# Two attentions and two expert layers on one core: gathers issued eight tiles ahead, fp32 shared up products, spline-weight pieces split between GpSimd and VectorE

## What is computed

```python
# x: (2, 16, 64, 128) = 2048 tokens of 128
# layer 0: x += local attention(layernorm(x)); x += Gelu experts(layernorm(x))
attn = softmax(einsum(q, kw) + pos_bias)          # 8 heads, window of 7 keys
hs = gelu(t @ sw1.T + sb1); shared = hs @ sw2.T + sb2       # 2 shared experts, 128 -> 512 -> 128
probs = softmax(t @ gate_w.T + gate_b); top_v, top_i = top_k(probs, 2)
hr = gelu(t @ rw1[e].T + rb1[e]); oe = hr @ rw2[e].T + rb2[e]  # 8 routed experts
# layer 1: x += window attention(layernorm(x)) with mask and pos_bias;
#          x += spline experts(layernorm(x)), 8 experts, two chosen per token
spline = einsum('nic,oic->no', b_splines(x), spline_w * scaler[..., None])
```

## Time and profile before

| | us |
|---|---|
| median of 3 runs | 1081.29 |
| lowest, highest | 1079.32, 1101.76 |
| the profiled execution | 1086.91 |
| its span in the profile | 1085.1 |
| TensorE busy | 859.6 (79%) |
| VectorE busy | 600.0 (55%) |
| ScalarE busy | 594.8 (55%) |
| GpSimd busy | 396.6 (37%) |
| moved by DMA | 157.42 MB, mean 145 GB/s |

### The profile page before, as it was taken

One profiled execution on the slowest core, in us unless ns is written; L12 is line 12 of the kernel. 1 busy time (PEld: TensorE's weight loads), 2 busy tenths in 40 slices (PEclk: granted clock), 3 DMA queues, 4 the chain that ended last, 5 costly groups with the idle time before them and its releaser, 6 DMA issues. The chain is left out here.

```text
span 1085.1 us, 22519 instructions
## 1 busy us (share of the span) xinstructions
PE 859.6 (79%) x7570; PEld 797.7 (74%) x7570; DVE 600.0 (55%) x1362; ACT 594.8 (55%) x1697; POOL 396.6 (37%) x407
## 2 busy tenths in 40 slices
PE   4684699754656534885698999999999999999993
PEld 3573588644545533674455999999999999999993
DVE  4563564331211344443393687887777777777762
ACT  4785443211212215885103878777777777777751
POOL 3997000343533423999001133233322333232111
PEclk9976599887988875666588999999999999999997
DMA  9362710246563349252506246442245353431000
GB/s 361 133 277 121 262 51 29 73 132 229 182 255 119 125 156 388 100 224 111 191 1 258 110 143 227 138 167 77 97 143 207 118 185 99 146 126 20 9 7 7
DMA packets 39171, 157.42 MB, mean 145 GB/s; under 512 B 5193, under 2 KB 23154, under 8 KB 31938
## 3 DMA queue, kind: packets, MB, share of 16 engines
q1 hardware_dynamic: 29746, 146.36, 36.1%
q0 software_dynamic: 9360, 10.23, 4.9%
HBM read 119.81 MB, written 36.77 MB: 144 GB/s over the span
## 5 line engine op out<-in xcount | busy, mean ns | idle before, releaser
L1472 PE MATMUL kan_ps_h<-kan_xf,kan_w 128*128 128x128 f32 x2496 | 304.3, 275 | 2.0 <-DMA kan_w<-w_dram 2.0
L1472 PEld LDWEIGHTS kan_ps_h<-kan_xf,kan_w 128*128 128x128 f32 x2496 | 291.2, 192 | 2.8 <-DMA kan_w<-w_dram 2.8
L1486 PE MATMUL kan_ps_y<-kan_w,kan_hf 128*128 128x128 f32 x1248 | 154.2, 277 | 8.3 <-DVE kan_hf L1624 8.3
L1486 PEld LDWEIGHTS kan_ps_y<-kan_w,kan_hf 128*128 128x128 f32 x1248 | 147.4, 194 | 8.8 <-issue 8.8
L1695 POOL DMA_INDIRECT out<-kan_y_sb,kan_slots_y x39 | 63.9, 1638 | 230.9 <-ACT kan_y_sb L1570 230.9
L796 ACT ACTIVATE f_hid<-f_ps_up,f_wt 128x128 f32<-128x128 f32 x156 | 44.5, 367 | 151.6 <-PE f_ps_up L737 151.6
L1616 DVE TENSOR_TENSOR kan_hfar<-kan_ht,kan_hfar 128x1024 f32<-128x1024 f32 x39 | 47.8, 1227 | 84.4 <-ACT kan_hnear L1533 84.4
L367 ACT ACTIVATE a_probs<-a_logits,a_below 128x70 f32<-128x70 f32 (+1 forms) x256 | 85.9, 351 | 0.0
L818 POOL DMA_INDIRECT y_dram<-f_y_sb,f_target x39 | 42.2, 1081 | 108.8 <-DVE f_y_sb L972 84.7
L1519 ACT ACTIVATE kan_ht<-kan_hu,kan_biases 128x256 f32<-128x256 f32 x156 | 66.2, 496 | 13.5 <-DVE kan_hu L1643 13.5
L811 POOL DMA_INDIRECT f_slot_x<-normed_dram,f_source x39 | 39.5, 1012 | 91.2 <-DVE f_source L952 79.6
(11 more groups left out here) (257 smaller groups left out, 1896.1 us busy)
## 6 DMA issues: line engine op xcount, KB each, us to landing
kan_w<-w_dram SPq DMA_DIRECT2D x16, 2304.0 KB, 8.9
sw_raw<-in_experts SPq DMA_DIRECT2D x8, 3456.0 KB, 12.4
f_wt<-in_experts SPq DMA_DIRECT2D x39, 514.0 KB
w_dram<-sw_raw SPq DMA_DIRECT2D x8, 2304.0 KB, 7.3
kan_w<-w_dram SPq DMA_DIRECT2D x16, 1152.0 KB, 5.2
w_dram<-sw_raw SPq DMA_DIRECT2D x8, 1152.0 KB, 11.2
sw_scal<-in_scalers SPq DMA_DIRECT2D x8, 384.0 KB, 13.4
f_ws<-in_experts SPq DMA_DIRECT2D x2, 514.0 KB, 4.2
```

What stands on the lines that cost most here:

```text
L1472: mm = eng.matmul(ps_h[n % 2][:, m, :], w12[n % 2][:, at:at + P], rhs, start=(c == 0), stop=(c == BASES))
L1486: mm = eng.matmul(ps_y[n % 2][:, :], lhs, w3[n % 2][:, i * P:(i + 1) * P], start=(i == 0), stop=(i == CH1 * FEAT - 1))
```

## The change

Five parts. (1) In the routed tiles GpSimd gathers eight tiles before it scatters one, with six buffers instead of four, and the gather stands ahead of the scatter in the loop. (2) The shared up products are one fp32 matmul instead of three fp32r passes; the splits on VectorE and ScalarE fall away, as do TensorE's wait for the small bias load. (3) The counts are made one step earlier, ahead of `go_down(0)`, and the lists three steps earlier. (4) In each attention GpSimd does two pieces an iteration (experts 0 and 2, then 5 and 7) and VectorE one (expert 1, then 6); stores 3 and 4 move to the start of the second attention, whose loads 6 and 7 wait for them. (5) The window bias table is made by GpSimd ahead of the second attention instead of by VectorE between routed tiles, and `w1` is loaded a block earlier.

```diff
-        X_BUFFERS = 4
+        X_BUFFERS = 6
...
-        COUNT_AT = 2
-        LIST_AT = STEPS - 1
+        COUNT_AT = 1
+        LIST_AT = 4
...
-                        for j, (wj, nj) in enumerate(PARTS):
-                            mm = eng.matmul(ps_up[c % 2][:, :], w_parts[e][wj][:, c * P:(c + 1) * P],
-                                            n_parts[nj][:, g * GROUP:(g + 1) * GROUP, :],
-                                            start=(j == 0), stop=(j == len(PARTS) - 1))
-                        mm.then_inc(up, 1)
+                        eng.matmul(ps_up[c % 2][:, :], ws[e][:, c * P:(c + 1) * P],
+                                   nT[:, g * GROUP:(g + 1) * GROUP, :], start=True, stop=True).then_inc(up, 1)
...
-                for n in range(X_BUFFERS):
+                for n in range(X_BUFFERS + 2):
                     gather_x(n)
                 eng.wait_ge(slots_ok, 1)
                 for n in range(SLOT_TILES):
+                    gather_x(n + X_BUFFERS + 2)
                     scatter_y(n)
-                    gather_x(n + X_BUFFERS)
...
                 for n in range(SLOT_TILES):
-                    if n < 9:
-                        prep.piece(eng, 3, 2 * n)
...
+                    if n < 2 * prep.PIECES:
+                        prep.piece(eng, 3 + n // prep.PIECES, n % prep.PIECES)
...
+    def gpsimd(self, eng, i):
+        for j in range(2 * (i - self.first), 2 * (i - self.first) + 2):
+            k, piece = divmod(j, self.prep.PIECES)
+            if 0 <= k < len(self.by_gpsimd):
+                self.prep.piece(eng, self.by_gpsimd[k], piece)
+
+    def vector(self, eng, i):
+        if 0 <= i - self.first < self.prep.PIECES:
+            self.prep.piece(eng, self.by_vector, i - self.first)
...
+                          Beside(prep, first=2, by_gpsimd=(0, 2), by_vector=1), x_arrivals=s_x)
...
                 def load1(eng):
-                    eng.dma_start(w1_sb[:, :], d["w1"]).then_inc(s_w1, 16)
...
+                    eng.dma_start(pos1[:, :, :], d["pos1"]).then_inc(s_tab, 16)
+                    eng.dma_start(mask1[:, :, :], d["mask1"]).then_inc(s_tab, 16)
                     prep.load(eng, 5)
+                    prep.store(eng, 3)
+                    prep.store(eng, 4)
+                    prep.load(eng, 6, 3)
+                    prep.load(eng, 7, 4)
...
+                          Beside(prep, first=3, by_gpsimd=(5, 7), by_vector=6, ahead=add_masks), stats)
```

More of the change, by code:

```diff
@@ L388, in _ @@
                     eng.memset(v[b][:, :, :], 0.0).then_inc(zeroed, 1)
+                beside.ahead(eng)
                 arrived(eng)
@@ L476, in _ @@
                     add_out(i - 6)
+                    beside.vector(eng, i)
                 eng.wait_ge(measured, TILES)
@@ L516, in gelu_experts @@
         nT = sb("nT", [P, TILES, P])
-        n_parts = [sb(f"n_part{j}", [P, TILES, P], F32R) for j in range(2)]
         shared_sum = nT
@@ L635, in _ @@
                 eng.dma_start(normed_dram[TOKENS:, :], xn[:, 0, :]).then_inc(saved, 16)
+                eng.wait_ge(zeroed, W_BUFFERS + 1)
+                eng.dma_start(shared_b2[0:SHARED, :], d["b2"][0:SHARED, :]).then_inc(s_b2, 16)
+                for s in to_clear:
+                    eng.sem_clear(s)
+                prep.load(eng, 3)
+                prep.load(eng, 4)
                 eng.wait_ge(lots_ok, 1)
@@ L644, in _ @@
                        .then_inc(in_w[n % W_BUFFERS], 16)
-                    if n == 14:
-                        prep.store(eng, 3)
-                    if n == 22:
-                        prep.load(eng, 4, 3)
                 for i in range(Y_BUFFERS):
@@ L1008, in _, with __init__, ahead @@
                 eng.wait_ge(measured, TILES)
+class Beside:
+    def __init__(self, prep, first, by_gpsimd, by_vector, ahead=None):
+        self.prep, self.first, self.by_gpsimd, self.by_vector = prep, first, by_gpsimd, by_vector
+        self.before = ahead
+    def ahead(self, eng):
+        if self.before is not None:
+            self.before(eng)
+    def gpsimd(self, eng, i):
[6 more added lines that the diff above has]
+            self.prep.piece(eng, self.by_vector, i - self.first)
 class SplineWeights:
@@ L1775, in load0 @@
                     eng.dma_start(pads0[:, :, :], d["pads0"]).then_inc(s_w0, 16)
-                    prep.load(eng, 0)
-                    prep.load(eng, 1)
-                    prep.store(eng, 0)
-                    prep.load(eng, 2, 0)
-                    prep.store(eng, 1)
-                    prep.store(eng, 2)
+                    for e in range(3):
+                        prep.load(eng, e)
+                    for e in range(3):
+                        prep.store(eng, e)
                     for e in range(3):
@@ L1853, in fill1, with add_masks @@
                 def fill1(eng, logits):
-                    pass
-                def beside1(eng, i):
-                    for j in range(3 * (i - 3), 3 * (i - 2)):
-                        if 0 <= j < 3 * prep.PIECES:
-                            prep.piece(eng, 5 + j // prep.PIECES, j % prep.PIECES)
+                    eng.wait_ge(s_biased, WINDOWS // 2)
+                def add_masks(eng):
+                    eng.wait_ge(s_tab, 32)
+                    shape = [P, PAIRS, 2, BLK]
+                    for n in range(WINDOWS // 2):
+                        eng.tensor_tensor(window_bias[:, n, :, :].rearrange("p (h b) k -> p h b k", b=2),
+                                          pos1[:, :, :].unsqueeze(2).to_broadcast(shape),
+                                          mask1[:, 2 * n:2 * n + 2, :].unsqueeze(1).to_broadcast(shape), ALU.add)\
+                           .then_inc(s_biased, 1)
                 w = {n: w1_sb[:, i * P:(i + 1) * P] for i, n in enumerate(("wq", "wk", "wv", "wo"))}
```

152 lines of the change are left out of this document (50 added, 102 removed).

## The result

The changed kernel takes 1017.2 us (median of 4 runs, 1016.4 to 1019.5) against 1080.3 for the kernel before: a ratio of 0.943, with a 95% interval of 0.940 to 0.946. The forecast was 1026, in a range of 994 to 1058. Some executions of a kernel take some per cent longer at a lower granted clock (of e1, one takes 1115.9 us at 0.853 and another 1079.8 at 0.885); the ratios, and the time given for the first experiment, leave them out.

A forecast was written before the change was run, and what follows sets the result against it. Late gathers, queued behind scatters waiting for y, were taken to bound the routed tiles, and GpSimd the attentions. Gelu layer -92, first attention +12, second +25 make -55, so 1081.3 becomes 1026 us, range 994 to 1058.

The forecast's parts named there:

- GpSimd is: Routed tiles: GpSimd is the next bound, 70 operations x 1.27 = 89 us, over TensorE's 83 us.
- above L = 6: Routed tiles, rival (b): L, a weight load's time until it lands, binds above 6 us; 1103 or more, chance 0.04.
- if L727 waits for `f_wt`: Routed tiles: a named sign that the prediction is wrong, line L727 waiting for the weights `f_wt`; no size given.
- GpSimd busy over 85% there: Routed tiles: expected sign in the changed profile, GpSimd over 85% busy with y rows 2.6 to 2.9 us apart.
- The 11 us of collisions: Routed tiles: scatters collide with VectorE's pieces, 0.3 us a tile (between 0 and 0.46), 11 us in all.
- 89 + 11: Routed tiles: GpSimd's 70 operations, 89 us, plus 11 us of collisions with VectorE, giving 100 us.
- The bounds of this sum, 103 and 65: Routed tiles, gain of 90: 103 without collisions and TensorE's 83 us carrying it, 65 at 3.3 us a tile.
- Rival (a): Routed tiles: the low clock keeps the gain, 4.24 us a tile, layer gains about 29, time 1089; chance 0.06.
- nothing gained, nothing lost: Shared part: a step's eight fp32 instructions take 3.47 us against 3.43 for twelve fp32r passes, no change at 2.4 GHz.
- I take 4.65 a tile, hardly better than 4.68: First attention: tile interval 4.65 us (bounds 4.3 and 4.9), as GpSimd's and VectorE's pieces collide.
- would delay the start by 8: Second attention: GpSimd's table work, 10 us, hides in VectorE's wait for a load; uncovered it delays the start by 8.
- the 5.6 us of the profiled execution over its median: Sum: the profiled execution before, 1086.9, is 5.6 over the median, so -55 is taken from 1081.3, giving 1026.

The follow-up runs named there:

- e1: Changed kernel with only GpSimd's order in the routed tiles put back: four gathers ahead, then scatter(n) and gather(n+4), six buffers kept; 1088.0 us, ratio 1.010.
- e5: Changed kernel with five buffers for the routed weights instead of four; 1018.6 us, ratio 0.935.
- e9: Changed kernel with only the first eight gathers (later tiles compute on rows left in the buffers) and five routed weight buffers; 1003.6 us, ratio 0.925.
- e3: Changed kernel without VectorE's 36 pieces of experts 3 and 4 in the routed tiles, whose weights are stored unscaled; 1021.4 us, ratio 0.936.
- e4: Changed kernel with only the first eight gathers, tiles 8 to 38 computing on rows that stay in the buffers; 1022.5 us, ratio 0.936.
- e6: Changed kernel with all three experts of each attention on GpSimd, none on VectorE; loads, stores and tables in the changed kernel's order; 990.5 us, ratio 0.912.
- e8: As e7, with VectorE's pieces in iterations 5 to 16, three in two iterations, and GpSimd's share and the last stores' order changed; 1000.4 us, ratio 0.920.
- e10: Changed kernel with its split of pieces, but VectorE's first-attention pieces from iteration 4, stores and loads reordered, five weight buffers; 990.4 us, ratio 0.912.
- e13: As e10, with GpSimd's normalise ahead of add_bp, VectorE's pieces from iteration 5 in both attentions, store 6 last, beside route; 978.6 us, ratio 0.903.
- e7: Changed kernel with store 3 behind routed tile 26 and load 6 behind the loads of the results, instead of in the second attention; 1012.1 us, ratio 0.933.
- e2: Changed kernel with four row buffers and a lead of six tiles instead of six buffers and eight tiles; 1023.4 us, ratio 0.938.

## Why the prediction was right, and where not

**The bound and the routed tiles.** Right in the main: the order of GpSimd's queue made the gathers late, and without that edit no gain is left (e1), though the other edits of this layer took some 28 us of the stretch by themselves, for which the prediction has no term. Foreseen 107.5 us, and 2 more for stretches at the low clock, to the loads of the results; measured 305.4 - 200.57 = 104.8. The reason given for the 2.6 us a tile was half of it. The step "GpSimd is" the next bound failed: the weight loads bind beside it. The prediction lets them bind "above L = 6", but they do at 4.8 us from issue to use, since its sum for four tiles leaves out the 0.9 us between the down product and the issue, and the waits themselves. Its own sign of being wrong, "if L727 waits for `f_wt`", came in 23 of 39 tiles (the trace names no releaser; e5 and e9 tell it), and its "GpSimd busy over 85% there" did not: 68.98 of 95 us from 205 to 300, 73%. The 11 us of collisions were charged to a path that does not feel them (e3). That 89 + 11 came out at the right length is luck: the load's way over four buffers has nearly the same one. Only e4, e5 and e9 together tell the two apart. The bounds of this sum, 103 and 65, do not follow from its terms: 39 x 2.12 + 7.5 = 90.2 would be a gain of 109, 39 x 3.3 + 7.5 = 136.2 one of 63. The measured 94 lies inside either pair.

**Clock.** Rival (a) fell: the granted clock of the routed stretch is 1.00, against 0.83 before and 0.89 in e1, which has the waits again. So the 2 us for low-clock stretches were not needed. The profiles give the granted clock as a share of full speed only, and the prediction's GHz are in no run; its two states are: eight instructions of an up product take 1.06 us and 1.92 us.

**Shared part.** 82.9 us to the first routed product instead of 84.6, so -1.7; foreseen -2. That is luck: two errors cancel in it. The step "nothing gained, nothing lost" failed: I compared the busy time of a step of before, 3.43, which has its last product's tail in it, with a rate from start to start, 3.47. Like by like a step's eight instructions are busy 3.85 us and twelve passes 3.43, so eight steps cost 3.4 us more.

```profile
161.89 3.85 PE L676 MATMUL f_ps_up<-f_nT,f_ws 128*128 128x512 f32 x8
```

So the other edits of this part saved about 5 us, not 2; which of them, no run here separates.

**First attention,** +5.4 for +12, at the edge of its bounds; the other profiles of the same block give +4.6 to +11.4, so part of the difference is the one execution. The wait was as forecast (the load lands at 27.76, "about 27"). First transposes at 36.13, 1.7 later than the 34.4. The end is 19.3 us behind the last transposes, for 21.0. The step that failed is the interval: "I take 4.65 a tile, hardly better than 4.68" against a measured (98.36 - 36.13)/15 = 4.15, and 4.10 to 4.50 over all nine profiles. I had counted GpSimd's saving of 1.23 us and then given it all to collisions. What the runs give for the same block is 4.69 with three pieces on GpSimd (e6), 4.89 with two and one and a half (e8), and with two and one at a free start 4.51 (e10), no less than behind the wait. If a piece of VectorE held GpSimd up for its own 0.68 us, 3.45 + 0.68 would be 4.13 (an estimate), the low end of the 4.10 to 4.50; the 4.65 went beyond it. No row of the prediction shows what a piece costs GpSimd: its 1.41 us are of `norm`, which has one tensor operand, where a piece has two. In e13 a `normalise` that began under a piece took 1.50 us instead of 1.04. And a collision need not cost time: e3 takes away the scatters' (at most 998 ns instead of 1499), and its tile takes 2.63 us for 2.60.

**Second attention,** +22.8 for +25. VectorE's piece starts 41.6 us after the block's start for 40, the first transposes 47.8 for 45, the last 115.7 for 117.8, and the end is 20.7 behind them for 21.2. The interval is 4.53 instead of 4.9 in the mean, of which 4.9 is right up to the tenth tile and 3.9 holds behind it. The prediction gives no reason for the 4.9 but the 4.96 of before; in the trace it is the loop, and e13 shows that GpSimd's and VectorE's mutual waits would hold it at 4.65 without one. That GpSimd's table work without cover "would delay the start by 8" is not borne out: in e6, where no piece of VectorE waits, the first transposes come 28.6 us after the block's start against 25.4 before, 3.2 later. In e7 they come at 32.5, but there the table work itself begins 7.9 us after the start instead of 4.3, waiting for the mask, whose load is queued behind load 6. The 117.8 for the last transposes is a slip: 45 + 14 x 4.9 + 4 is 117.6.

**The sum.** -67.7 on the span for -55: 4 us of the difference come from the Gelu layer, 6.6 from the first attention (in most other profiles less), 2.2 from the second. Of these 12.7 us the median shows 9 (1026 against 1017.2): I took the 5.6 us of the profiled execution over its median as lasting, and the changed kernel's is over it by 2.3 only.

## What to carry to other kernels

A gather with a queue that also waits for results must stand ahead of that wait (put back behind it, the routed stretch takes 171.6 us for 105.5, e1); how many buffers it has matters less than its place (188.4 us for 187.7 and 186.4, e2). When the wait is gone, look for two limits side by side before naming one: an edit that relieves only one may show next to nothing. And an interval read from one profile is one reading: repeat it before building on it. Work handed to an idle engine brings its own waits along: its first piece stands in that engine's order (waits of 16.45 and 20.33 us here), and a load or store that is late holds everything queued behind (8.47 us in e7, 5.47 in e13); three pieces on the full engine beat two and one here by 27 us, and with the waits moved the two are level (e6 and e10, ratio 0.912 each). That the shared work is the better way is not shown: e13, at 0.903, has a fifth weight buffer and other moves that three pieces on GpSimd were never given.

## What the runs showed of the hardware

In the changed kernel a VectorE piece of 128x512 takes 0.68 us in the routed tiles (680 to 683 ns, 16 in the trace), with no GpSimd piece beside it. In the second attention one took 1.72 us beside two pieces of GpSimd (377.66 to 379.38; GpSimd's two ran from 376.33 for 2.50 us): it ended 0.55 us behind GpSimd's second. In the second attention of e13 VectorE's pieces took 1.52 to 1.84 us and GpSimd's 1.26 to 1.29. In the other direction, in e13, `normalise` began at 343.16 under VectorE's piece (342.11 to 343.76) and took 1.50 instead of 1.04 us, and `norm`, begun at 343.68 under `normalise`, took 1.06 instead of 0.33 and ended with it. The two with two tensor operands ended their own time alone behind the other's end, to about 0.15 us: 378.83 + 0.68 = 379.51 for 379.38, and 343.76 + 1.04 = 344.80 for 344.66. `norm` ended only 0.08 us behind `normalise`, sooner than its own 0.33 would have it.

In e7 a load behind a store in one queue came late by about the store's time. The 0.53 MB load behind a store of 3.54 MB was issued at 263.22 and its up product started at 276.14, 12.9 us later, after a wait of 8.47 us; the store's own time is estimated at 8.6, from its 3.54 MB and the 0.41 MB/us that the earlier trace rows come to at a full DMA share. In the changed kernel, with no store between the loads, it is 4.8 us in the median of 23 tiles from the issue to the up product that waited, with gathers, scatters and a second small load on the same engines. No row shows the landing itself.
